# Bias of the up projection added to tile copies on ScalarE instead of by a matmul, with a new order of steps, in a fused adapter and attention kernel

## The chip, the cores and the metric

The kernel runs on one core of a Trainium2 chip. The metric is the device time of one execution in microseconds, lower is better; the figure compared is the median of several executions. A profile of one further execution goes with it.

## The reference, cut to what matters

Input x has 32 sequences of 32 tokens with 256 features. Each sequence has a role (1 or 2, clamped to 0 to 2), which picks the weights of three adapters. Four layers follow one another: an adapter (layer 0), attention and two MLPs (layer 1), an adapter (layer 2), an adapter (layer 3).

```python
def adapter(role, x, W_down, b_down, W_up, b_up, gamma, beta):
    h = gelu(einsum('bsh,bhk->bsk', x, W_down[role]) + b_down[role][:, None, :])
    u = einsum('bsk,bkh->bsh', h, W_up[role]) + b_up[role][:, None, :]
    y = x + u
    yn = (y - mean(y)) * rsqrt(var(y) + 1e-5)
    return yn * gamma[role][:, None, :] + beta[role][:, None, :]

def layer1(x, ...):
    attn = softmax((x @ Wq) @ (x @ Wk).T / 16)
    ao   = (attn @ (x @ Wv)) @ Wp + bp
    cms  = gelu(ao @ cW1 + cb1) @ cW2 + cb2 + one_hot(code)
    mod  = gelu(concat(ao, cms) @ mW1 + mb1) @ mW2 + mb2
    return clip(x + cms + mod, 0, 1)
```

## The kernel before, in words

The 1024 tokens are cut into 8 tiles of 128 tokens (4 sequences). The kernel sorts the sequences so that six tiles, the plain ones (0, 1, 2, 3, 6, 7), hold one role each; tiles 4 and 5, the mixed ones (MESSY), hold what is left and two roles, so they multiply with two sets of weights and mask the result. Layer 0 takes the tiles in the order 0, 1, 2, 3, 6, 7, 4, 5, layers 2 and 3 in the order of their numbers.

All engines walk through one list of steps, `plan()`. Each engine does its own part of a step and skips those in which it has none, so the list sets the order on every engine, and semaphores tie the engines together. The steps of an adapter tile are:

- load: gathered rows of x are transposed on TensorE into a bank and copied by ScalarE to xA (layer 0); in layer 2 VectorE clips x1T into xA. Layer 3 reads zB, which turn has written.
- down: TensorE puts x back into the bank in token order (two transposing matmuls, L741), adds b_up by a matmul with a one-hot matrix (L743), and computes the down product into the bank's other half (L748). ScalarE applies the Gelu with b_down (L940 for a plain tile, L945 for a mixed one), VectorE masks the mixed tiles (L1282).
- up: TensorE adds the up product to the bank (L764). VectorE takes statistics of a row (L1256, L1257), GpSimd raises the variance to the power -0.5 (L1514).
- center: VectorE subtracts the mean and scales, into yA (L1321).
- turn: TensorE transposes yA (L774), ScalarE applies gamma and beta into x1T or zB (L956, L968), for mixed tiles VectorE does it in two products (L1300, L1302).
- close and finish: in layer 3 VectorE writes the normed tile in two instructions (L1340, L1347), and GpSimd stores tiles 0 to 5 by an indirect DMA (L1529), SyncE and ScalarE store tiles 6 and 7.

The steps of layer 1 are split, project, scores, values, probs and mix (attention), hidden and outer (the MLPs, each matmul in three passes over high and low parts, L636 to L638), and weights (VectorE splits an MLP matrix into such parts, L1247, L1248). The hidden steps of the last phase, (3, 0) to (3, 7), and the outer steps (3, 0) to (3, 7) alternate with adapter tiles of layers 2 and 3. outer(3, 7) is the last matmul work of layer 1; VectorE then adds the result to x1T (L1432), from which tiles 6 and 7 of layer 2 start.

Adapter weights lie in two rings of four slots. SyncE fetches them in the order of its own program (L560, L563): for each slot it waits until the up step that last used it is done. For layers 2 and 3 it fetches in turn one pass of layer 2 and one of layer 3. The last two tiles have slots of their own (wd_last, wu_last).

For the bias matmul, VectorE builds the one-hot matrix `hot` for all eight tiles (first_hot and rest, L1137, L1189, L1191) and splits b_up of the three layers into high and low rows (first_bias for layer 0, L1216, L1218; late_biases for layers 2 and 3, L1230, L1232). SyncE loads those rows (bu_rows) ahead of everything but the first three loads, once GpSimd has cleared the tile (constants 3). chunk_vecs holds, per plain tile, the vectors of its role that ScalarE uses as bias and scale: b_down, gamma, beta; it comes from a matmul over vec_rows with 11 rows per role.

The program's names in the rows: bank is PSUM, stage the slots of MLP and attention matrices, x_tok gathered rows, g_h and g_l the high and low parts of the Gelu output, mvA and mvB the mean and variance of layers 0 and 2 and of layer 3.

Of the kernel before, what the change touches and what calls it, by code (L numbers as in the profile page):

```python
# [16 lines left out]
F32 = mybir.dt.float32  # L17
# [7 lines left out]
P = 128  # L25
# [25 lines left out]
PER_ROLE = 11  # L51
# [5 lines left out]
XSLOTS, YSLOTS, WSLOTS, TSLOTS = 3, 4, 4, 8  # L57

# [55 lines left out]
def plan():  # L114
# [7 lines left out]
        ("down", 0, 3), ("center", 0, 1), ("up", 0, 2), ("late_biases",), ("turn", 0, 0), ("center", 0, 2),
        ("up", 0, 3), ("load", 0, 7), ("seq_vecs",), ("turn", 0, 1), ("weights", 0, 0), ("center", 0, 3),
        ("load", 0, 4), ("down", 0, 6), ("down", 0, 7), ("turn", 0, 2), ("up", 0, 6), ("up", 0, 7), ("turn", 0, 3),
        ("center", 0, 6), ("split", 0, 0), ("load", 0, 5), ("down", 0, 4), ("center", 0, 7), ("token_tables",),
        ("turn", 0, 6), ("down", 0, 5), ("project", 0, 0), ("weights", 0, 1), ("turn", 0, 7), ("up", 0, 4),
        ("project", 0, 1), ("split", 1, 0), ("center", 0, 4), ("up", 0, 5), ("codes",), ("turn", 0, 4),
        ("center", 0, 5), ("scores", 0), ("values", 0, 0), ("probs", 0), ("values", 0, 1), ("turn", 0, 5),
        ("split", 1, 1), ("weights", 1), ("mix", 0), ("weights", 2), ("project", 1, 0), ("project", 1, 1),
        ("values", 1, 0), ("scores", 1), ("probs", 1), ("values", 1, 1), ("hidden", 0, 0), ("hidden", 0, 1),  # L130
        ("hidden", 0, 2), ("hidden", 0, 3), ("hidden", 0, 4), ("weights", 3), ("mix", 1), ("hidden", 0, 5),
# [5 lines left out]
        ("down", 2, 0), ("down", 2, 1), ("hidden", 3, 1), ("load", 2, 2), ("up", 2, 0), ("center", 2, 0),  # L137
# [1429 lines left out]
```

## Time and profile before

| | us |
|---|---|
| median of 3 runs | 202.34 |
| lowest, highest | 200.64, 202.97 |
| the profiled execution | 198.34 |
| its span, first to last instruction | 196.6 |

The profiled execution is one more run than the three. Its time holds 1.74 us ahead of and behind the span. The profile names for every instruction its start, its length and what ended the idle time before it. The recorded ends of matmuls are modelled: in the rows of time their lengths overlap, while the chain counts a step from start to start.

### The profile page before, as it was taken

What the parts mean: (1) busy time and instruction counts of PE and PEld (TensorE: products, weight loads), DVE (VectorE), ACT (ScalarE), POOL (GpSimd) and SP (SyncE); (2) the same over time, 40 slices, a digit from 0 to 9 for tenths busy, and PEclk for the clock granted to TensorE, in tenths of its full rate; (3) what the DMA queues carried; (4) which work ended last, traced back from release to release, by engine and by line L of the source; (5) the groups of instructions that cost most, each with busy time, mean ns of one, the idle gap of its engine ahead of it and who ended that gap; (6) DMA issues with size and microseconds to landing.
All of it is one profiled execution on the core that took longest, in us unless ns stands there. A gap on an engine that the chain in (4) does not pass through costs nothing.

```text
span 196.6 us, 3109 instructions
## 1 busy us (share of the span) xinstructions
PE 184.1 (94%) x1031; PEld 157.7 (80%) x1031; DVE 114.4 (58%) x283; ACT 80.7 (41%) x164; POOL 44.2 (22%) x74
## 2 busy tenths in 40 slices
PE   7877999989999999999999999999999999999960
PEld 7755878878988888778888888888888989999840
DVE  2994998989648807983193522041442146569972
ACT  0733656544698405672045543003546242222420
POOL 8472848200000006000140000000110012234552
PEclk9999999999999999999999999999999999999995
DMA  3687389996300230330000060000100005433002
GB/s 110 224 243 242 97 259 294 245 312 187 107 3 8 100 107 0 107 110 0 0 0 3 0 196 18 0 0 3 55 0 0 3 0 141 125 85 107 28 27 80
DMA packets 18585, 17.82 MB, mean 91 GB/s; under 512 B 2049, under 2 KB 16970, under 8 KB 18570
## 3 DMA queue, kind: packets, MB, share of 16 engines
q1 hardware_dynamic: 16720, 14.60, 24.3%
q0 software_dynamic: 1024, 2.37, 4.5%
q10 hardware_dynamic: 826, 0.67, 1.1%
q8 instruction: 8, 0.13, 0.3%
q14 instruction: 7, 0.06, 0.1%
HBM read 16.58 MB, written 1.05 MB: 90 GB/s over the span
## 4 chain that ended last, share of the span: by engine, by line
PE 79%; DVE 8%; DMA 5%; issue 3%; ACT 2%; POOL 1%; ACTq 0%; DVEq 0%; POOLq 0%
PE bank L636 20%; PE bank L638 19%; PE bank L637 19%; PE bank L748 5%; PE bank L764 5%; DMA stage<-in_L_cond_Wq 2%; PE bank L741 2%; PE bank L815 2%; PE bank L804 2%; DMA x_tok<-in_x,from_row_i 2%; PE bank L774 1%; DVE yA L1321 1%; PE bank L743 1%; DMA out<-yB,from_row_i 1%; DVE cms_l L1423 1%
## 5 line engine op out<-in xcount | busy, mean ns | idle before, releaser
L1402 DVE TENSOR_TENSOR g_l<-g_full,g_h 128x512 fp32r<-128x512 f32 x32 | 21.8, 690 | 36.1 <-ACT g_h L1028 36.0
L1025 ACT ACTIVATE g_full<-bank,vecs 128x512 f32<-128x512 f32 x32 | 22.1, 691 | 43.5 <-PE bank L638 39.9
L1514 POOL TENSOR_TENSOR mvA<-mvA,power 128x1 f32<-128x1 f32 x16 | 9.4, 589 | 72.0 <-DVE mvA L1257 72.0
L1028 ACT ACTIVATE g_h<-bank,vecs 128x512 fp32r<-128x512 f32 x32 | 22.0, 686 | 0.0
L1541 POOL TENSOR_TENSOR x1T<-x1T,cms_full 128x512 f32<-128x512 f32 x4 | 6.0, 1497 | 57.4 <-DVE cms_full L1417 57.3
L636 PE MATMUL bank<-g_h,mw_h 128*128 128x256 f32 (+1 forms) x48 | 16.0, 334 | 0.0
L638 PE MATMUL bank<-g_h,mw_l 128*128 128x256 f32 (+1 forms) x48 | 15.3, 318 | 0.0
L637 PE MATMUL bank<-g_l,mw_h 128*128 128x256 f32 (+1 forms) x48 | 15.3, 318 | 0.0
L636 PE MATMUL bank<-ao_h,mw_h 128*128 128x512 f32 x32 | 13.1, 411 | 0.0
L636 PE MATMUL bank<-ao_h,cw_h 128*128 128x512 f32 x32 | 12.8, 400 | 0.1
L638 PE MATMUL bank<-ao_h,mw_l 128*128 128x512 f32 x32 | 12.5, 391 | 0.0
L637 PE MATMUL bank<-ao_l,mw_h 128*128 128x512 f32 x32 | 12.5, 390 | 0.0
L638 PE MATMUL bank<-cms_h,mw_l 128*128 128x512 f32 x32 | 12.5, 390 | 0.0
L638 PE MATMUL bank<-ao_h,cw_l 128*128 128x512 f32 x32 | 12.5, 390 | 0.0
L636 PE MATMUL bank<-cms_h,mw_h 128*128 128x512 f32 x32 | 12.5, 390 | 0.0
L637 PE MATMUL bank<-ao_l,cw_h 128*128 128x512 f32 x32 | 12.5, 390 | 0.0
L636 PE MATMUL bank<-g_h,cw_h 128*128 128x512 f32 x32 | 12.5, 389 | 0.0
L638 PE MATMUL bank<-g_h,cw_l 128*128 128x512 f32 x32 | 12.5, 389 | 0.0
L637 PE MATMUL bank<-cms_l,mw_h 128*128 128x512 f32 x32 | 12.5, 389 | 0.0
L637 PE MATMUL bank<-g_l,cw_h 128*128 128x512 f32 x32 | 12.4, 389 | 0.0
L1321 DVE TENSOR_SCALAR yA<-bank,mvA 128x256 f32<-128x256 f32 x16 | 8.6, 540 | 3.1 <-POOL mvA L1514 2.8
L1417 DVE TENSOR_TENSOR cms_full<-bank,target 128x512 f32<-128x512 f32 x4 | 2.8, 692 | 12.9 <-PE bank L638 12.9
(265 smaller groups left out, 442.8 us busy)
## 6 DMA issues: line engine op xcount, KB each, us to landing
stage<-in_L_cond_mW SPq DMA_DIRECT2D x6, 512.0 KB
stage<-in_L_cond_cW SPq DMA_DIRECT2D x4, 512.0 KB
wdA<-in_L_cond_W_down SPq DMA_DIRECT2D x14, 128.0 KB
wuA<-in_L_cond_W_up SPq DMA_DIRECT2D x14, 128.0 KB
wdB<-in_L_cond_W_down SPq DMA_DIRECT2D x12, 128.0 KB, 2.5
wuB<-in_L_cond_W_up SPq DMA_DIRECT2D x12, 128.0 KB, 2.8
wd_last<-in_L_cond_W_down SPq DMA_DIRECT2D x4, 128.0 KB, 2.3
wu_last<-in_L_cond_W_up SPq DMA_DIRECT2D x4, 128.0 KB, 2.5
```

The costliest lines, as they stand in the source:

```text
L636: pe.matmul(dst, w[0], x[0], start=first, stop=False)
L637: pe.matmul(dst, w[0], x[1], start=False, stop=False)
L638: return pe.matmul(dst, w[1], x[0], start=False, stop=last)
L741: pe.matmul(bank[b][:, m * P:(m + 1) * P], x[:, m, :], ident[:, :], start=(m == 0), stop=False, is_transpose=True, skip_group_check=True)
L748: mm = pe.matmul(bank[b][:, D + part * P:D + (part + 1) * P], wd[:, k, :], x[:, k, :], start=False, stop=(k == KD - 1), skip_group_check=True)
L764: mm = pe.matmul(dst, h[:, part, :], wu[:, :], start=False, stop=(part == len(turns) - 1), skip_group_check=True)
L1025: act.activation(g_full[n % 2][:, 0:width], bank[b][:, 0:width], ACT.Gelu, bias=bias)
L1028: act.activation(g[0][:, j, 0:width], bank[b][:, 0:width], ACT.Gelu, bias=bias).then_inc(g_high, 1)
L1321: dve.tensor_scalar(yA[k][:, :], bank[chain_bank(layer, c)][:, 0:D], mvA[:, k, 0:1], mvA[:, k, 2:3], ALU.subtract, ALU.mult).then_inc(norm ...
L1402: dve.tensor_tensor(g[1][:, j, 0:width], g_full[n % 2][:, 0:width], g[0][:, j, 0:width].bitcast(F32), ALU.subtract).then_inc(g_ready, 1)
L1514: pool.tensor_tensor(mv[:, k, 2:3], mv[:, k, 1:2], power[:, :], ALU.pow).then_inc(done, 1)
L1541: pool.tensor_tensor(half, half, cms_full[:, m, :], ALU.add).then_inc(sum_ready, 1)
```

## The change

1. Plain tiles no longer get b_up by a matmul. ScalarE writes a copy of the tile with b_up added (`shift`: two activations of 128 x 128, bias from chunk_vecs) into new tiles rA (layers 0 and 2) and rB (layer 3), three slots each. In layer 0 it reads the transposed x in the bank, behind the copy to xA, in layer 2 xA, in layer 3 zB, behind its own writing of zB in turn. A slot waits for the TensorE step that last read it.
2. On TensorE, down of a plain tile is only the down product; the two transposing matmuls now read rA or rB and stand in up, ahead of the up product and behind the wait for the Gelu.
3. Mixed tiles keep the transposing matmuls and the bias matmul in down. `hot` is built for them alone; first_hot and first_bias are gone, and late_biases treats all three layers.
4. vec_rows has 17 rows per role instead of 11; the six new ones are b_up. chunk_vecs, seq_vecs and vecs grow with it, and both matmuls over vec_rows wait for six more small loads.
5. SyncE loads Wp first, then the small rows, then the weights of tiles 0, 1, 2, 3, 6, 7 of layer 0, then the first MLP matrix (piece 0) and bu_rows.
6. `plan()` has a new order.

```diff
+BU = {0: 11, 2: 13, 3: 15}
+PER_ROLE = 17
...
             def load(layer, c):
...
+                take(b, *((xA_ready, n + 1) if c in MESSY else (rA_ready, like_done(0, c))))
...
             def down(layer, c):
...
+                plain = c not in MESSY
+                if not plain:
+                    pe.wait_ge(bu_ready, 1)
+                    pe.wait_ge(hot_ready, 1)
+                    for m in range(KD):
+                        pe.matmul(bank[b][:, m * P:(m + 1) * P], x[:, m, :], ident[:, :], start=(m == 0), stop=False,
+                                  is_transpose=True, skip_group_check=True)
+                    pe.matmul(bank[b][:, 0:D], hot[:, c - MESSY[0], :], bu[:, (0, 2, 3).index(layer), :], start=False,
+                              stop=True, skip_group_check=True)
...
             def up(layer, c):
...
+                if c not in MESSY:
+                    r, ready, n, back = shifted(layer, c)
+                    pe.wait_ge(ready, n)
+                    for m in range(KD):
+                        tr = pe.matmul(bank[chain_bank(layer, c)][:, m * P:(m + 1) * P], r[:, m, :], ident[:, :],
+                                       start=False, stop=False, is_transpose=True, skip_group_check=True)
+                    tr.then_inc(back, 1)
...
+            def shift(layer, c, x):
+
+                r, ready, n, back = shifted(layer, c)
+                if n > RSLOTS:
+                    act.wait_ge(back, n - RSLOTS)
+                for m in range(KD):
+                    ins = act.activation(r[:, m, :], x[m], ACT.Identity,
+                                         bias=chunk_vecs[:, BU[layer] + m, full_column(c):full_column(c) + 1])
+                ins.then_inc(ready, 1)
...
-            def first_bias():
-
-                dve.wait_ge(bu_in, 16)
-                dve.tensor_copy(bu_high[:, 0, :], bu_rows[:, 0, :]).then_inc(bu_high_ready, 1)
...
+                dve.wait_ge(bu_in, 3 * 16)
+                dve.tensor_copy(bu_high[:, :, :], bu_rows[:, :, :]).then_inc(bu_high_ready, 1)
...
     return [
...
-        ("close", 3, 1), ("finish", 3, 0), ("load", 2, 5), ("down", 2, 4), ("up", 3, 2), ("outer", 3, 5),
...
+        ("up", 3, 1), ("load", 2, 5), ("turn", 2, 3), ("close", 3, 1), ("finish", 3, 1), ("outer", 3, 5),
```

TensorE, right behind the last matmul of outer(3, 7), before. xA_150 and xA_148 are tiles 6 and 7 of layer 2, zB_158 and wdB_135 tile 3 of layer 3, wuA_128 and wuA_129 the up weights of tile 5 of layer 2.

```order
L741 MATMUL bank<-ident,zB_158 128x128 x2
L743 MATMUL bank<-bu,hot 128x256
L748 MATMUL bank<-zB_158,wdB_135 128x128 x2
L774 MATMUL bank<-ident,yA_154 128x128 x2
L764 MATMUL bank<-wuA_128,hA_152 128x256
L764 MATMUL bank<-wuA_129,hA_152 128x256
L764 MATMUL bank<-wuB_139,hB_161 128x256
L741 MATMUL bank<-ident,xA_150 128x128 x2
L743 MATMUL bank<-bu,hot 128x256
L748 MATMUL bank<-xA_150,wd_last_8_140 128x128 x2
```

The same place now.

```order
L786 MATMUL bank<-wuA_130,hA_151 128x256
L786 MATMUL bank<-wuA_131,hA_151 128x256
L786 MATMUL bank<-wuA_128,hA_152 128x256
L786 MATMUL bank<-wuA_129,hA_152 128x256
L763 MATMUL bank<-zB_158,wdB_135 128x128 x2
L763 MATMUL bank<-xA_150,wd_last_8_140 128x128 x2
L763 MATMUL bank<-xA_148,wd_last_9_141 128x128 x2
L796 MATMUL bank<-ident,yA_154 128x128 x2
L780 MATMUL bank<-ident,rB_240 128x128 x2
L786 MATMUL bank<-wuB_139,hB_161 128x256
```

The up products of tile 4 (wuA_130, wuA_131) have come behind the last outer step. The three down steps have neither transposing nor bias matmuls, and up of tile 3 of layer 3 has the transposing ones, from rB_240.

VectorE from the clipping of tile 7 of layer 2 (xA_148) on, before. zB_159 is tile 4 of layer 3, yA_155 and yB_167 are tile 5 of layer 2 and tile 3 of layer 3.

```order
L1268 TENSOR_SCALAR xA_148<-x1T 128x256
L1300 TENSOR_TENSOR zB_159<-bank,seq_vecs 128x256
L1302 TENSOR_TENSOR zB_159<-zB_159,seq_vecs 128x256
L1256 BN_STATS statsA<-bank 128x6
L1257 BN_AGGR mvA<-statsA 128x2
L1256 BN_STATS statsB<-bank 128x6
L1257 BN_AGGR mvB<-statsB 128x2
L1321 TENSOR_SCALAR yA_155<-bank,mvA 128x256
L1340 ISA
L1340 SCALAR_TENSOR_TENSOR yB_167<-bank,mvB,table_gamma_172 128x256
```

The same place now. yA_154 is tile 4 of layer 2, yB_166 tile 2 of layer 3.

```order
L1298 TENSOR_SCALAR xA_148<-x1T 128x256
L1284 BN_STATS statsA<-bank 128x6
L1285 BN_AGGR mvA<-statsA 128x2
L1352 TENSOR_SCALAR yA_154<-bank,mvA 128x256
L1371 ISA
L1371 SCALAR_TENSOR_TENSOR yB_166<-bank,mvB,table_gamma_172 128x256
L1352 TENSOR_SCALAR yA_155<-bank,mvA 128x256
L1331 TENSOR_TENSOR zB_159<-bank,seq_vecs 128x256
L1333 TENSOR_TENSOR zB_159<-zB_159,seq_vecs 128x256
L1284 BN_STATS statsB<-bank 128x6
```

The centring of tile 4 and the first product of tile 2 now stand between xA_148 and zB_159; before, both stood ahead of the last outer step's result. In the whole stretch from the clipping of tile 6 to the statistics of tile 4 of layer 3 there are now one statistics pair, one centring, one first and one last product more than before.

SyncE from its third load to the first adapter weights, before.

```order
L536 DMA role_col_i<-in_itok_B_1546 32x1
L581 DMA bu_rows<-in_L_cond_b_up 6x1x256 x3
L583 DMA stage_122<-in_L_cond_Wp 128x2x256
L548 DMA stage_123<-in_L_cond_cW 128x1024
L587 DMA vec_rows<-in_L_cond_gamma 3x128 x2
L587 DMA vec_rows<-in_L_cond_beta 3x128 x2
L554 TENSOR_LOAD chunk_role_i
```

The same place now.

```order
L548 DMA role_col_i<-in_itok_B_1546 32x1
L591 DMA stage_122<-in_L_cond_Wp 128x2x256
L595 DMA vec_rows<-in_L_cond_b_up 3x128 x2
L595 DMA vec_rows<-in_L_cond_gamma 3x128 x2
L595 DMA vec_rows<-in_L_cond_beta 3x128 x2
L595 DMA vec_rows<-in_L_cond_b_up 3x128 x4
L566 TENSOR_LOAD chunk_role_i
```

bu_rows and the 512 KB matrix (cW) have gone behind the weights of six tiles.

## Rows read from the trace of the kernel before

**Rows 1.** The page, part 1: busy us, share of the span, instructions.
```profile
PE 184.1 (94%) x1031; PEld 157.7 (80%) x1031; DVE 114.4 (58%) x283; ACT 80.7 (41%) x164; POOL 44.2 (22%) x74
```

**Rows 2.** Busy time by stage: stretch, its length, busy of each engine.
```profile
12.00:51.85 39.85, 36.40 (x248) 31.58 (x249) 33.11 (x99) 19.46 (x49) 14.80 (x19) 1.00 0.79 232
51.85:130.60 78.75, 78.60 (x354) 64.71 (x353) 40.09 (x56) 35.61 (x57) 5.99 (x4) 1.00 0.13 42
130.60:176.90 46.30, 46.30 (x291) 41.53 (x290) 19.31 (x47) 16.63 (x35) 6.58 (x10) 1.00 0.15 44
176.90:196.60 19.70, 12.94 (x88) 11.04 (x86) 14.10 (x39) 4.59 (x13) 8.91 (x13) 0.89 0.19 60
```

**Rows 3.** The chain that ended last: start, us, what (x2: pieces of one step).
```profile
133.50 0.22 PE bank L741 x2
133.72 0.12 PE bank L743
133.84 0.44 PE bank L748 x4
...
157.48 0.86 PE bank L764 x4
...
187.50 0.74 issue
188.23 1.04 POOL out L1529
189.30 0.59 POOL mvB L1514
```

**Rows 4.** TensorE in order of time: start, length, line, operands.
```profile
14.01 0.41 PE L719 MATMUL bank<-ident,x_tok 128*128 128x128 f32 x2 [0.47 <-issue]
...
176.80 0.38 PE L741 MATMUL bank<-ident,zB 128*128 128x128 f32 x2
```

**Rows 5.** SyncE's fetches for a released slot, and the landing of wd_last.
```profile
170.37 0.37 SPq L560 DMA_DIRECT2D wdB<-in_L_cond_W_down  x1
171.37 0.38 SPq L560 DMA_DIRECT2D wdA<-in_L_cond_W_down  x1
...
DMA to landing us min/median/max: 2.1/2.3/2.6
```

**Rows 6.** VectorE behind the last outer step, in order of time.
```profile
177.52 0.49 DVE L1268 TENSOR_SCALAR xA<-x1T 128x256 f32<-128x256 f32 x2
178.00 0.42 DVE L1300 TENSOR_TENSOR zB<-bank,seq_vecs 128x256 f32<-128x256 f32 x1
...
178.87 0.43 DVE L1256 BATCH_NORM_STATS2 statsA<-bank 128x6 f32<-128x256 f32 x1
179.45 0.39 DVE L1256 BATCH_NORM_STATS2 statsB<-bank 128x6 f32<-128x256 f32 x1
...
180.22 0.54 DVE L1321 TENSOR_SCALAR yA<-bank,mvA 128x256 f32<-128x256 f32 x1 [0.15 <-POOL mvA L1514]
180.68 0.48 DVE L1340 SCALAR_TENSOR_TENSOR yB<-bank,mvB,table_gamma 128x256 f32<-128x256 f32 x1
...
185.56 0.43 DVE L1256 BATCH_NORM_STATS2 statsB<-bank 128x6 f32<-128x256 f32 x1
```

**Rows 7.** GpSimd's second of two stores in a row.
```profile
177.23 0.98 POOL L1529 DMA_INDIRECT out<-yB,from_row_i  x1 [0.30 <-issue]
```

**Rows 8.** ScalarE and VectorE: activations, and VectorE's one-hot and bias passes.
```profile
15.75 0.37 ACT L923 COPY xA<-bank 128x256 f32<-128x256 f32 x1 [1.59 <-PE bank L719]
17.31 0.62 ACT L940 ACTIVATE hA<-bank,chunk_vecs 128x128 f32<-128x128 f32 x2 [1.19 <-PE bank L748]
...
185.78 1.50 ACT L968 ACTIVATE zB<-bank,chunk_vecs 128x128 f32<-128x128 f32 x4 [0.67 <-PE bank L774]
...
22.00 0.28 DVE L1191 CAST hot<-hot_col 128x256 fp32r<-128x256 f32 x1
23.22 0.72 DVE L1230 CAST bu_high<-bu_rows 128x512 fp32r<-128x512 f32 x1
23.97 0.75 DVE L1232 SCALAR_TENSOR_TENSOR bu<-bu_high,low_row,bu_rows 128x512 fp32r<-128x512 f32 x1
```

More of the change, by code:

```diff
@@ L122, in plan @@
[L122 to L126, printed above, removed]
@@ new lines, in plan @@
+        ("turn", 0, 0), ("up", 0, 2), ("weights", 0, 0), ("load", 0, 6), ("up", 0, 3), ("center", 0, 2),
+        ("down", 0, 6), ("load", 0, 7), ("seq_vecs",), ("late_biases",), ("turn", 0, 1), ("center", 0, 3),
+        ("up", 0, 6), ("down", 0, 7), ("load", 0, 4), ("turn", 0, 2), ("up", 0, 7), ("token_tables",),
+        ("turn", 0, 3), ("center", 0, 6), ("split", 0, 0), ("load", 0, 5), ("center", 0, 7), ("down", 0, 4),
+        ("down", 0, 5), ("turn", 0, 6), ("project", 0, 0), ("weights", 0, 1), ("up", 0, 4), ("turn", 0, 7),
@@ L150, in plan @@
-        ("finish", 3, 5), ("close", 3, 6), ("down", 3, 7), ("finish", 3, 6), ("up", 3, 7), ("close", 3, 7),
-        ("finish", 3, 7),
+        ("down", 2, 2), ("turn", 2, 1), ("hidden", 3, 5), ("down", 3, 0), ("hidden", 3, 6), ("load", 2, 3),
+        ("outer", 3, 0), ("up", 2, 2), ("up", 3, 0), ("hidden", 3, 7), ("outer", 3, 1), ("down", 2, 3),
+        ("close", 3, 0), ("center", 2, 2), ("outer", 3, 2), ("up", 2, 3), ("down", 3, 1), ("turn", 2, 2),
+        ("outer", 3, 3), ("center", 2, 3), ("finish", 3, 0), ("outer", 3, 4), ("load", 2, 4), ("down", 3, 2),
@@ L284, in build @@
         role_row_of = place("role_row_of", [P, 1], F32)
-        hot_col = place("hot_col", [P, FULL], F32)
         hot_rest = place("hot_rest", [P, 2 * WB], F32)
-        hot = place("hot", [P, WIN, P], F32R)
+        hot = place("hot", [P, len(MESSY), P], F32R)
+        rA = [place(f"rA{i}", [P, KD, P], F32) for i in range(RSLOTS)]
         x1T = place("x1T", [P, KD, N], F32)
@@ L327, in build @@
         cms_full = place("cms_full", [P, KD, HALF], F32, scratch)
+        rB = [place(f"rB{i}", [P, KD, P], F32, scratch + 4 * KD * P * i) for i in range(RSLOTS)]
         at[0] = max(at[0], early_end)
@@ L748, in down @@
                         mm = pe.matmul(bank[b][:, D + part * P:D + (part + 1) * P], wd[:, k, :], x[:, k, :],
-                                       start=False, stop=(k == KD - 1), skip_group_check=True)
+                                       start=(plain and k == 0), stop=(k == KD - 1), skip_group_check=True)
                 mm.then_inc(done, 1)
@@ L972, in turn2 @@
                 ins.then_inc(zB_ready, 1)
+                if c == 0:
+                    act.wait_ge(cms_ready, 2 * KD)
+                    act.wait_ge(sum_ready, 2 * KD)
+                act.wait_ge(zB_ready, like_done(2, c))
+                shift(3, c, [zB[c % XSLOTS][:, m, :] for m in range(KD)])
             def values(h, q):
@@ L1267, in load @@
                 dve.wait_ge(downA_ps, i - XSLOTS + 1)
+                if c >= XSLOTS and c - XSLOTS not in MESSY:
+                    dve.wait_ge(rA_ready, like_a(2, c - XSLOTS))
                 dve.tensor_scalar(xA[i % XSLOTS][:, :, :], x1T[:, :, c * P:(c + 1) * P], 0.0, 1.0,
```

123 lines of the change are left out of this document (59 added, 64 removed).

## The prediction, made before the changed kernel ran

> **What bounds the kernel now.** I read the busy shares first, then busy time by stage, then the chain that ended last, then the rows in time around the two places where TensorE waits. TensorE is busy 94% of the span, VectorE 58%, ScalarE 41% [rows 1]. By stage it falls apart [rows 2]. From 12 to 51.85 us (adapters of layer 0, attention) TensorE is busy 36.40 of 39.85 us, VectorE 33.11: 3.45 us idle. From 51.85 to 130.60 it is full (78.60 of 78.75), from 130.60 to 176.90 as well (46.30 of 46.30). After that, where only adapter tiles are left, it is busy 12.94 of 19.70 us, and VectorE 14.10. So a matmul taken out before 176.9 pays in full, one taken out behind it only if the chain there runs over TensorE. That chain, over the last 10 us, alternates VectorE, GpSimd's store of one tile and GpSimd's power for the next: 0.74 us from a finished tile to the store, the store, and only then the power at 189.30 [rows 3]. The granted clock is 1.00 in the three long stages.
>
> **The profiled run and the median.** The profiled execution took 198.34 us, 1.74 more than its span of 196.6; the median of the runs is 202.34. I sum differences against the span and add them to the median.
>
> **TensorE's part.** A plain tile loses its bias matmul: 0.12 us in the chain, 18 of them (6 plain tiles, 3 layers), 2.16 us. The two transposing matmuls (0.22 a pair) stay, but stand in up instead of down, and there behind the wait for the Gelu, so they hide under nothing: 0.34 less ahead of each Gelu, 0.22 more behind it [rows 3].
>
> From the first matmul of hidden(3,0) to the end of outer(3,7) at 176.80 [rows 4] TensorE is full, so the sum counts: 7 plain down steps there without bias, 7 x 0.12 = 0.84, and the two up matmuls of tile 4 of layer 2 now stand behind outer(3,7), 0.86 [rows 3]. The last outer ends 0.84 + 0.86 = 1.70 us earlier, of which only 0.84 is work gone.
>
> Could weights be late there? SyncE asks for a slot's weights only once the slot's last up is done, in a fixed order, and layer 3's first fetch for tile 5 (behind up(3,2)) stands ahead of layer 2's second for tile 5: 1.00 us between the two [rows 5]. Now only down(2,4) (0.22 + 0.12 + two weight pairs of 0.44 = 1.22) and outer(3,6) (12 matmuls as wide as the bias one, 1.44) stand between up(3,2) and down(2,5), whose second half is needed 0.65 + 1.22 + 1.44 + 0.22 + 0.12 + 0.44 = 4.09 us after up(3,2) began [rows 3]. The fetch is issued 0.65 + 0.16 (end of the step to the result, 0.38 less 0.22 [rows 3, 4]) + 1.00 = 1.81 after that and lands 2.3 later (2.1 to 2.6) [rows 5]: 4.11. Just in time; I take 0, and up to 0.3 for the upper end.
>
> **VectorE behind the last outer.** Steps between starts [rows 6]: statistics 0.58 (178.87 to 179.45), centring 0.46, two products for a mixed tile 0.87 (178.00 to 178.87), xA 0.25, first product of a finished tile 0.48, last the same form, mask 0.40 (it is of the form of those products, 0.42 long). From the end of outer(3,7) to the statistics of tile 4 of layer 3 it is 185.56 - 176.80 = 8.76 now. In the new order VectorE starts with x1T and xA, waits for up(2,4) until 1.07 (0.86, the same 0.16, and the hand-over), and then has in a row: 5 statistics (2.90), xA (0.25), 4 centrings (1.84), 2 first products (0.96), 2 mixed tiles (1.74), 2 last products (0.96), 2 masks (0.80): 9.45. Each of TensorE's and ScalarE's results for it comes earlier than its turn by my count (for example the Gelu of tile 4 at about 7.6, its mask's turn at 8.8). So the statistics start at 10.52, 1.76 later against the end of the outer. VectorE was waiting before where it now works: statistics and centring of tile 4 of layer 2, a first and a last product were done before the outer ended.
>
> GpSimd then has two stores (tiles 2 and 3) right ahead of the power of tile 4. A store takes 1.04 [rows 3], the next starts 0.30 behind it and takes 0.98 [rows 7]. Tile 2 is finished at 8.32, its store starts 0.8 later (0.74 and the hand-over, [rows 3]), at 9.12, the second at 10.46 and is over at 11.44; the power could have started about 0.7 behind the statistics (0.58 and the hand-over), at 11.24: 0.20 late. From there on the order is the one of before to the end. Tail: -1.70 + 1.76 + 0.20 = +0.26.
>
> **The start.** ScalarE gets 18 pairs of 128-wide activations. It has not run this form; the nearest is the Gelu with a bias, a pair 0.62 [rows 8], which I take; the dearer bound is the scaled pair, 1.50 for four, 0.75 [rows 8]. 18 x 0.62 = 11.2 us on an engine busy 80.7: no bound in itself. In layer 0 they stand between the copy of x and the Gelu. Down is 0.34 shorter and up 0.22 longer, -0.12 once. Then VectorE leads: it is busy 33.11 of the stage's 39.85 us [rows 2], and its pass over the late biases ends just where the next centring starts [rows 8]. The early hot and bias work (four instructions) went from a stretch where it ran ahead; what counts is the copy of hot_col, 0.28 gone, and the late bias pass, now 768 wide instead of 512: 0.72 + 0.75 become half as much again, +0.73 [rows 8]. Start: -0.12 - 0.28 + 0.73 = +0.33, and since TensorE is full from project on, it stays. Bounds: nothing below -3.45 (all the idle time of the stage, [rows 2]) and nothing above 6 x 0.62 = 3.7, if every pair stood in the chain. SyncE: the first matrix (512 KB) goes behind the weights of six tiles, b_up gets six small row copies ahead of the two vector transposes; the queue starts Wp at once instead of behind the wait for bu_rows, so these are issued before it waits for the roles, and cost nothing. Weights(3) ahead of hidden(0,0) puts two VectorE instructions before the first g_l, which outer(0,0) needs only eight hidden steps later: 0.
>
> Sum: +0.26 + 0.33 = +0.6: 202.34 + 0.6 = 202.9 us (a profiled span of about 197.2).
>
> **Rivals.**
> B, TensorE's sum. If VectorE's queue behind the last outer packs tighter than rows 6 say, or the end hangs on TensorE after all, the 18 matmuls pay in full: 202.34 - 2.16 = 200.2. For it: the tail's chain does touch TensorE at several tiles. Against: 5 us and more of TensorE idle in the tail [rows 2].
> C, queued transfers. At the start ScalarE stands idle 1.59 us before xA of the second tile and 1.19 before the first Gelu, though the matmuls it names had long been issued [rows 8]. If that is the 512 KB matrix in front of x and the weights, it goes with the new order: up to 2.78 less the new pair, 2.16. Then 202.9 - 2.16 = 200.7. Against: the transpose of that tile starts at 14.01 [rows 4], so its data was there. The Trainium skill, DMA: Bandwidth & Descriptors, section Queues, rings and completion order, says that a transfer's semaphore lands only after every earlier write of that DMA engine, across its queues: by that rule the new order would free the gathers' semaphores, and the time is this rival's. No row here shows it directly.
> D, ScalarE's queue, slower. It is in order, and each new pair stands ahead of the next copy, Gelu or x1T. If in layer 0 five of six pairs hold up the chain, 5 x 0.62 = 3.1 on top of mine less the 0.33 that VectorE would then hide: 202.9 + 3.1 - 0.3 = 205.7. It decides from the point where ScalarE's idle time ahead of a Gelu is under 0.62; now it is 1.19 and 1.59 at the first tiles [rows 8], and ScalarE is busy 19.46 of 39.85 us [rows 2]. The Trainium skill, TensorE: Matmul & The Clock Gate, section on the array's architecture, calls ScalarE's queue strictly first in, first out; by it nothing overtakes such a pair, and this rival stands.
>
> **How the numbers follow.** Mine 0.46, B 0.17, C 0.15, D 0.17, 0.05 for something else. About 1% (2 us) is what a measurement of this kernel tells from no change, its runs lying 2.3 us apart. Faster by over 1% (under 200.3): most of B, a third of C, 0.23. Slower (over 204.4): D and the upper end of mine, 0.21. Within: 0.56. The range 199.5 to 206.0 takes in B, C and D; mine alone is 201.6 to 204.2.
>
> **What would show it.** Right: outer(3,7) ends 1.4 us earlier in the span (1.70 less 0.33); VectorE without a gap over 0.3 us from 1.1 us after it until the statistics of tile 4; project(0,0) 0.3 us later in the span; the new pair takes 0.62 to 0.75 us. Wrong: ScalarE named ahead of TensorE's gaps before 30 us (D), those two gaps gone (C), a tail shorter than 20 us behind the last outer (B), a stall at down(2,5).

## The result, and the profile after

| | before | after |
|---|---|---|
| median of 20 runs each, taken on one chip | 200.36 us | 203.61 us |
| lowest, highest | 198.38, 203.10 | 201.57, 208.63 |
| ratio after to before, 95% interval | | 1.0171 (1.0137 to 1.0205) |
| the profiled execution, its span | 198.34, 196.6 | 202.39, 200.4 |

The changed kernel is slower by 1.7%, 3.25 us between the medians, where the forecast said +0.6. The 202.34 on which the forecast stood was the median of three runs only; twenty runs of the same kernel give 200.36. Ratios, here and below, compare only the executions in the faster of the two states that an execution can be in, while medians and extremes are of all of them, so the two need not agree to the last digit.

Part 1 of the page of the changed kernel answers to [rows 1].

```profile
PE 184.3 (92%) x1013; PEld 156.9 (78%) x1013; DVE 112.9 (56%) x278; ACT 91.6 (46%) x200; POOL 44.9 (22%) x74
```

ScalarE is 10.9 us busier and TensorE has 18 matmuls fewer, as planned. Yet TensorE is busy 0.2 us longer, not 2.2 us shorter: some of its steps took more time each. The busy time by stage shows where (the stretches are cut at the same steps as in [rows 2]; columns: stretch, its length, busy of each engine, granted clock, DMA share, GB/s).

```profile
12.00:54.96 42.96, 38.09 (x246) 32.24 (x246) 34.22 (x101) 23.02 (x63) 15.56 (x19) 0.96 0.81 232
54.96:133.70 78.74, 78.58 (x354) 64.74 (x353) 40.17 (x56) 35.56 (x57) 6.00 (x4) 1.00 0.13 41
133.70:178.66 44.96, 44.74 (x280) 39.97 (x279) 17.36 (x42) 21.74 (x51) 6.20 (x9) 1.00 0.16 48
178.66:200.40 21.74, 13.27 (x88) 11.21 (x86) 15.50 (x44) 7.18 (x21) 9.90 (x13) 0.91 0.16 49
```

Against [rows 2] the first stretch is 3.11 us longer, the second equal, the third (46.18 us from hidden(3,0) to the end of outer(3,7) before, cut at 130.62 and 176.80) 1.22 shorter, the last (19.8 before) 1.94 longer: +3.8 together. The granted clock of the first is 0.96, where it was 1.00. That of the last (0.91, before 0.89) falls only behind TensorE's last step and costs nothing: it is 1.00 until 192 us before and until 196 after, and that step starts at 190.06 and 192.13.

**The start.** TensorE in order of time, before, then after.

```profile
6.03 1.07 PE L692 MATMUL bank<-ident,stage 128*128 128x128 f32 x8 [0.77 <-DMA stage<-in_L_cond_Wq]
...
17.73 1.13 PE L764 MATMUL bank<-wuA,hA 128*128 128x256 f32 x4 [0.32 <-ACT hA L940]
...
30.97 0.47 PE L636 MATMUL bank<-x_h,wqk_h 128*128 128x512 f32 x1 [0.17 <-issue]
```

```profile
6.88 1.06 PE L706 MATMUL bank<-ident,stage 128*128 128x128 f32 x8 [1.34 <-DMA stage<-in_L_cond_Wq]
...
14.96 1.35 PE L763 MATMUL bank<-xA,wdA 128*128 128x128 f32 x8
16.15 0.38 PE L733 MATMUL bank<-ident,x_tok 128*128 128x128 f32 x2
18.61 0.46 PE L780 MATMUL bank<-ident,rA 128*128 128x128 f32 x2 [2.08 <-ACT hA L980]
18.89 1.04 PE L786 MATMUL bank<-wuA,hA 128*128 128x256 f32 x2
...
33.55 0.47 PE L650 MATMUL bank<-x_h,wqk_h 128*128 128x512 f32 x1 [0.18 <-issue]
```

Three things are to be seen. Wq lands later: the first transposes start at 6.88, 0.85 later than before. Then TensorE stands idle for 2.08 us until the first Gelu. And behind that wait an up step takes 1.04 us instead of the 0.60 of an undisturbed one: the clock has fallen from 2.4 to 1.2 GHz. The same view as above for two short stretches, behind the wait and in it, has the granted clock at 0.50 and 1.00:

```profile
18.90:22.30 3.40, 3.40 (x14) 2.50 (x12) 1.65 (x5) 1.33 (x6) 0.88 (x2) 0.50 0.65 202
16.00:18.60 2.60, 0.53 (x5) 0.29 (x4) 0.61 (x2) 0.47 (x3) 0.86 (x1) 1.00 0.95 287
```

project(0,0) starts at 33.55 us instead of 30.97, 2.58 later. ScalarE at the same place, after:

```profile
15.43 0.63 ACT L944 ACTIVATE rA<-bank,chunk_vecs 128x128 f32<-128x128 f32 x2
18.19 0.62 ACT L980 ACTIVATE hA<-bank,chunk_vecs 128x128 f32<-128x128 f32 x2 [2.13 <-remote]
```

The down product for the first Gelu was issued at 14.96 and the second one ended by 16.3. ScalarE, free since 16.06, started the Gelu at 18.19, and the profile names no engine ("remote") as the releaser. [Rows 8] held the same gap in two pieces, 1.59 and 1.19.

Another 0.5 us is lost between project(0,0) and the first mix. ScalarE and VectorE each copy half of the scores; VectorE, after:

```profile
40.78 0.43 DVE L1333 TENSOR_TENSOR x1T<-x1T,seq_vecs 128x256 f32<-128x256 f32 x1
41.13 0.54 DVE L1352 TENSOR_SCALAR yA<-bank,mvA 128x256 f32<-128x256 f32 x1
41.58 0.56 DVE L1401 COPY dots<-bank 32x128 f32<-32x128 f32 x2
```

ScalarE's copy starts at 41.09, VectorE's 0.49 later, behind the products of a mixed tile and a centring; before, both started at 38.46.

**Around the last outer steps.** TensorE and SyncE, after.

```profile
172.18 0.38 PE L780 MATMUL bank<-ident,rB 128*128 128x128 f32 x2
...
176.67 0.71 PE L763 MATMUL bank<-xA,wdA 128*128 128x128 f32 x4 [0.22 <-DMA wdA<-in_L_cond_W_down]
...
178.66 1.89 PE L786 MATMUL bank<-wuA,hA 128*128 128x256 f32 x8
```

```profile
174.00 0.56 SPq L572 DMA_DIRECT2D wdA<-in_L_cond_W_down  x1
```

up(3,2) starts at 172.18; the weights for the second half of down(2,5) are asked for 1.82 us later and arrive 2.67 us after that, 0.39 us too late (176.67 against 176.28, when the first half is done).

**The tail.** VectorE and GpSimd, after; [rows 3, 6, 7] are the same places before.

```profile
179.72 0.43 DVE L1284 BATCH_NORM_STATS2 statsA<-bank 128x6 f32<-128x256 f32 x1
...
186.15 0.48 DVE L1378 SCALAR_TENSOR_TENSOR yB<-yB,mvB,table_beta 128x256 f32<-128x256 f32 x1
...
188.64 0.43 DVE L1284 BATCH_NORM_STATS2 statsB<-bank 128x6 f32<-128x256 f32 x1
```

```profile
187.44 1.63 POOL L1560 DMA_INDIRECT out<-yB,from_row_i  x1 [0.40 <-issue]
189.37 0.98 POOL L1560 DMA_INDIRECT out<-yB,from_row_i  x1 [0.31 <-issue]
190.35 0.59 POOL L1545 TENSOR_TENSOR mvB<-mvB,power 128x1 f32<-128x1 f32 x1
```

The statistics of tile 4 of layer 3 start 9.98 us behind the last outer (8.76 before) and the power 11.69 behind it (9.51 before, 186.31 less 176.80), held by the second store. From there to the end the tail gives 0.24 us back.

### The profile page after: what moved, and what is told of

Its sections match the earlier page's. It is cut to its first block, busy times and chain, and to the rows that moved or that the text cites. A ratio compares the mean times of both kernels' runs of the same rounds, so it can differ in the third digit from the quotient of the medians.

```text
span 200.4 us, 3123 instructions
## 1 busy us (share of the span) xinstructions
PE 184.3 (92%) x1013; PEld 156.9 (78%) x1013; DVE 112.9 (56%) x278; ACT 91.6 (46%) x200; POOL 44.9 (22%) x74
## 4 chain that ended last, share of the span: by engine, by line
PE 72%; DVE 10%; DMA 5%; issue 4%; ACT 3%; POOL 2%; another core or an unknown queue 1%; SPq 0%; ACTq 0%; DVEq 0%; POOLq 0%
PE bank L650 19%; PE bank L652 18%; PE bank L651 18%; PE bank L786 4%; PE bank L763 3%; DMA stage<-in_L_cond_Wq 3%; PE bank L837 2%; PE bank L826 2%; DMA wdA<-in_L_cond_W_down 1%; PE bank L720 1%; POOL out L1560 1%; DVE mw_l L1276 1%; PE bank L780 1%; PE bank L796 1%
## 5 line engine op out<-in xcount | busy, mean ns | idle before, releaser
L650 PE MATMUL bank<-g_h,mw_h 128*128 128x256 f32 (+1 forms) x48 | 15.7, 326 | 0.0
L650 PE MATMUL bank<-ao_h,cw_h 128*128 128x512 f32 x32 | 12.8, 399 | 0.2
L944 ACT ACTIVATE rA<-xA,chunk_vecs 128x128 f32<-128x128 f32 x12 | 4.1, 393 | 16.0 <-DVE xA L1298 16.0
L1082 ACT CAST cms_h<-cms_full 128x512 fp32r<-128x512 f32 x4 | 2.5, 622 | 17.9 <-DVE cms_full L1448 9.7
```

The source lines that it names most:

```text
L650: pe.matmul(dst, w[0], x[0], start=first, stop=False)
L944: ins = act.activation(r[:, m, :], x[m], ACT.Identity, bias=chunk_vecs[:, BU[layer] + m, full_column(c):full_column(c) + 1])
```

## The experiments

My theory for the start at this point: the new order of loads makes Wq late, and the long wait for the first Gelu lets the clock fall. Rivals: the added pairs in ScalarE's queue, or the new order of steps. L numbers in rows are those of each run's own kernel.

**1. The moved work alone.** The changed kernel with both old orders: the steps of before without first_hot, of which two places stand here, and the loads of run 2.

```diff
-        ("chunk_vecs",), ("vectors",), ("load", 0, 0), ("fold", 1, 1), ("load", 0, 1), ("down", 0, 0),
+        ("chunk_vecs",), ("vectors",), ("sort_rest",), ("load", 0, 0), ("fold", 1, 1), ("load", 0, 1),
...
-        ("up", 3, 2), ("down", 2, 4), ("outer", 3, 6), ("down", 2, 5), ("outer", 3, 7), ("load", 2, 6), ("up", 2, 4),
+        ("close", 3, 2), ("finish", 3, 2), ("outer", 3, 6), ("down", 2, 5), ("outer", 3, 7), ("down", 3, 3),
```

> The changed kernel with the old order of steps and the old order of loads: only the work moved from TensorE to ScalarE is left of the change. Theory 1 (the start is lost to the new load order: Wq lands at 6.75 instead of 5.90 us, and then to a TensorE clock that falls because the first Gelu comes late): project(0,0) starts at 31.0 to 31.5 us, as before, the outer stretch is 0.84 us shorter, ratio to before 0.990 to 1.000. Theory 2 (ScalarE's queue: the added pairs hold up the Gelus of layer 0): project(0,0) still 2 us or more later, ratio 1.008 or more. Theory 3 (the order of steps makes the loss at the start): reads as theory 1 here, and differs in the next run.

Measured: median 199.56 against 199.81, ratio 1.005 (0.9995 to 1.0104).

```profile
6.28 1.07 PE L705 MATMUL bank<-ident,stage 128*128 128x128 f32 x8 [0.59 <-DMA stage<-in_L_cond_Wq]
...
31.63 0.47 PE L649 MATMUL bank<-x_h,wqk_h 128*128 128x512 f32 x1 [0.16 <-issue]
...
151.79 0.71 PE L762 MATMUL bank<-xA,wdA 128*128 128x128 f32 x4 [0.36 <-ACT zB L1007]
```

Wq is 0.25 late, though it is loaded as before: with the loads of before the wait for it ended anywhere from 6.00 to 6.46 in the seven traces of this case (runs 1, 2, 7 and 10 to 12 and the kernel before). project(0,0) is 0.66 late, so 0.41 us at the start belong to the moved work; the rest of the 2.58 does not. VectorE shows where they arise: the two passes over the late biases and then the next centring, in this run, and that centring in the kernel before, where the passes start at 23.22 [rows 8].

```profile
23.37 0.96 DVE L1258 CAST bu_high<-bu_rows 128x768 fp32r<-128x768 f32 x1
...
25.30 0.54 DVE L1351 TENSOR_SCALAR yA<-bank,mvA 128x256 f32<-128x256 f32 x1
```

```profile
24.64 0.54 DVE L1321 TENSOR_SCALAR yA<-bank,mvA 128x256 f32<-128x256 f32 x1
```

The wider passes take 1.93 us instead of 1.42, 0.51 more; ahead of them this run is 0.15 late, and behind them 0.66 until project(0,0).

From project to mix it takes 11.31 us, as before; every run with the new order there took 11.6 to 11.8. So that half microsecond is the order's. The moved work gains nothing either: the stretch of hidden(3,0) to outer(3,7) is only 0.23 us shorter. Taken step by step, TensorE saves 1.42 us of bias matmuls (seven), pays 0.56 more for the transposing ones (0.22 a pair where 0.14 was paid in down), and loses 0.64 around the wait for zB shown above, which ScalarE writes later with its longer queue. Its end is 0.4 longer (20.0 us against 19.6; here and in runs 3, 8 and 11 the stretches that begin or end with outer(3,7) are measured to the modelled end of its last matmul, 0.15 behind the start of the next step, which the table above takes: 21.6 for the changed kernel, and 45.1 for the stretch ahead). Between the two nothing is left.

**2. The old order of loads.**

```diff
+            sp.wait_ge(constants, 3)
+            for m, w in enumerate(("L0_cond_b_up", "L2_cond_b_up", "L3_cond_b_up")):
+                sp.dma_start(bu_rows[0:2 * R, m, :],
...
             sp.dma_start(square("p"), a["L1_cond_Wp"].rearrange("(k p) n -> p k n", p=P)).then_inc(square_in["p"], 16)
+            piece(0)
...
-                if n == 5:
-                    piece(0)
```

> The changed kernel with SyncE's old order of loads (bu_rows, Wp and piece 0 ahead of the small rows), new order of steps. Theory 1: the wait for Wq is over at about 5.9 instead of 6.75, project(0,0) starts 0.85 us earlier than in the changed kernel at least (32.7), and if the late Gelu goes too, at 31 to 31.5; ratio to before 1.003 to 1.013. Theories 2 and 3: no change against the changed kernel, ratio 1.017.

Measured: ratio 1.0157 (1.0049 to 1.0266).

```profile
6.12 1.06 PE L705 MATMUL bank<-ident,stage 128*128 128x128 f32 x8 [1.17 <-DMA stage<-in_L_cond_Wq]
...
32.66 0.47 PE L649 MATMUL bank<-x_h,wqk_h 128*128 128x512 f32 x1 [0.18 <-issue]
```

Wq is on time and project(0,0) 0.89 us earlier than in the changed kernel. That is the part of the loads, and all of it, for in this execution too the clock fell, at two waits of TensorE of 1.39 and 1.07 us. As the size of that part 0.85 is at the upper end: the six traces with the new loads and no wait added have 6.73 to 6.88, on average 0.6 behind the seven of run 1.

**3. The old order of steps from load(2,0) on.**

```diff
-        ("down", 2, 0), ("hidden", 3, 1), ("up", 2, 0), ("center", 2, 0), ("down", 2, 1), ("load", 2, 2),
+        ("load", 2, 0), ("load", 2, 1), ("hidden", 3, 0), ("down", 2, 0), ("down", 2, 1), ("hidden", 3, 1),
...
-        ("up", 3, 2), ("down", 2, 4), ("outer", 3, 6), ("down", 2, 5), ("outer", 3, 7), ("load", 2, 6), ("up", 2, 4),
+        ("turn", 2, 3), ("close", 3, 2), ("finish", 3, 2), ("outer", 3, 6), ("down", 2, 5), ("outer", 3, 7),
```

> The changed kernel with the old order of steps from load(2,0) on, new order ahead of it. Theory: the start stays as in the changed kernel (project(0,0) at 33.5); the 0.4 us stall at down(2,5) goes, the stretch from the end of outer(3,7) to the end of the span is 19.8 to 20.2 us instead of 21.7, while outer(3,7) ends 0.84 us earlier than before against hidden(3,0) instead of 1.22: together 1.1 to 1.5 us less than the changed kernel, ratio to before 1.010 to 1.012. Rival (the tail's order gives and takes the same): ratio 1.017 as the changed kernel.

Measured: median 202.05 of four runs, lowest 200.46 (the changed kernel's lowest: 201.57); too few runs for a ratio with an interval. TensorE in the profile:

```profile
18.50 0.44 PE L780 MATMUL bank<-ident,rA 128*128 128x128 f32 x2 [1.66 <-ACT hA L980]
...
32.22 0.47 PE L650 MATMUL bank<-x_h,wqk_h 128*128 128x512 f32 x1 [0.18 <-issue]
```

In that profile, 198.5 us of span, TensorE waited 1.66 us for the first Gelu instead of 2.08 and the clock did not fall, and project(0,0) stands at 32.22 with the new order ahead of it. Of the 1.33 us between that and 33.55, 0.11 are there already at the first up step (18.50 against 18.61). The fall is worth the other 1.22: from that step to project(0,0) it takes 13.72 here, 13.72 in run 4 and 13.71 in run 1, all without a fall, and 14.94 in the changed kernel and 14.86 in run 2, both with one of 3.4 us. It is not in every execution. The stall at down(2,5) is gone, and the rest behind the last outer takes 20.0 us instead of 21.6 (19.6 before). What is left of the tail's loss shows here; ScalarE, then TensorE:

```profile
187.94 0.69 ACT L944 ACTIVATE rB<-zB,chunk_vecs 128x128 f32<-128x128 f32 x2
188.54 0.79 ACT L1008 ACTIVATE zB<-bank,chunk_vecs 128x128 f32<-128x128 f32 x2
189.36 0.69 ACT L944 ACTIVATE rB<-zB,chunk_vecs 128x128 f32<-128x128 f32 x2
189.96 0.35 ACT L980 ACTIVATE hB<-bank,chunk_vecs 128x128 f32<-128x128 f32 x1
```

```profile
190.35 0.44 PE L780 MATMUL bank<-ident,rB 128*128 128x128 f32 x2 [1.67 <-ACT hB L980]
```

Two new pairs stand ahead of the Gelu of tile 6, and TensorE waits 1.67 us for it, where it waited 0.46 before.

**4. Filler matmuls in the wait for the first Gelu.**

```diff
-        ("sort_rest",), ("down", 0, 1), ("load", 0, 2), ("sort_codes",), ("fold_low", 1), ("up", 0, 0), ("up", 0, 1),
+        ("down", 0, 1), ("load", 0, 2), ("sort_codes",), ("fold_low", 1), ("warm", 4), ("up", 0, 0), ("up", 0, 1),
```

> The changed kernel with eight 128x128 filler matmuls on TensorE ahead of up(0,0), where it waits 2.1 us for the first Gelu. They compute nothing of the result. Theory 1: the granted clock stays at 1.00 between 18 and 24 us, the steps there take what they take at 2.4 GHz (0.60 for an up pair instead of 1.04), and project(0,0) starts 1.0 to 1.7 us earlier, ratio to before 1.008 to 1.012. Rival (the fallen clock is covered by VectorE and ScalarE, which set the pace there): same as the changed kernel, 1.017.

Measured: ratio 1.0114 (1.0006 to 1.0221), lowest 201.50.

```profile
16.70 1.06 PE L658 MATMUL bank<-warm 128*128 128x128 f32 x8
18.49 0.44 PE L780 MATMUL bank<-ident,rA 128*128 128x128 f32 x2 [0.74 <-ACT hA L980]
18.76 0.60 PE L786 MATMUL bank<-wuA,hA 128*128 128x256 f32 x2
...
32.21 0.47 PE L650 MATMUL bank<-x_h,wqk_h 128*128 128x512 f32 x1 [0.18 <-issue]
```

With a shorter gap the up step takes 0.60 again, and project(0,0) stands where it stood in run 3 without a fall: 1.34 us earlier than in the changed kernel. Alone the filler proves little, since run 3 has no fall without it; the two together give the price of a fall. The fillers do not bring the Gelu nearer, and the lowest time is no better than the changed kernel's 201.57, which had no fall either by its mean clock (0.989).

**5. Wp no earlier than before.**

```diff
+            sp.wait_ge(constants, 3)
             sp.dma_start(square("p"), a["L1_cond_Wp"].rearrange("(k p) n -> p k n", p=P)).then_inc(square_in["p"], 16)
```

> The changed kernel with one wait added in SyncE: Wp is issued only when GpSimd has cleared bu_rows (constants 3, about 3.2 us), as before. Theory 1a (what delays Wq is Wp, issued 3.2 us earlier than before and moved at the same time as Wq, Wk): the wait for Wq ends at 5.9 to 6.3 us. Rival 1b (the six small loads of b_up rows, or the place of piece 0, delay it): 6.8 us as in the changed kernel.

Measured: one run, 203.28.

```profile
6.13 1.06 PE L707 MATMUL bank<-ident,stage 128*128 128x128 f32 x8 [0.44 <-DMA stage<-in_L_cond_Wq]
```

The early issue is what makes Wq late: with Wp issued at 3.23 instead of 2.19 us, beside the 512 KB of Wq and Wk, the wait ends 0.75 earlier, and the new place of the first MLP matrix, kept here, has no part in it. The wait held back the small loads behind Wp too (from 2.66 to 3.65), so the run does not part the two; the sizes, 256 KB against 1.5 KB for each of the six new ones, speak for Wp. The run as a whole was no faster, because the clock fell for 6.8 us at a wait of 2.93 us.

**6 and 7. Weights held back,** in the changed kernel and in the kernel before.

```diff
+                if n == 3:
+                    sp.wait_ge(hA_ready, 1)
                 adapter_weights(0, n)
```

> The changed kernel with one wait added in SyncE: the weights of the fourth tile and all after them are asked for only once the first Gelu is done. Theory Q (the first Gelu comes 2.1 us late because the results it waits for are reported late while loads queue up): the Gelu starts before 17.3 us instead of 18.2, TensorE's wait there is under 1.2 us, the clock does not fall; project(0,0) at 31 to 31.8 instead of 33.5, ratio to before 1.003 to 1.010. Rival (the late Gelu has nothing to do with the loads behind it): the Gelu at 18.1 to 18.2, and the weights held back may cost something more, ratio 1.017 or above.

> The kernel before with the same wait added. Theory Q: ScalarE's two idle stretches of 1.59 and 1.19 us ahead of the second xA and of the first Gelu shrink to under 1 us together, project(0,0) 1 to 2 us earlier than 31.0, ratio 0.990 to 0.997. Rival: same as before, or slower by up to 1 us where the held weights come late.

Measured: ratio 1.0247 (1.019 to 1.0303) and 0.9963 (0.9932 to 0.9994). The Gelu starts at 17.82 and at 17.66 (Wq was 0.4 later in the latter than in [rows 8]'s run), so with no weights asked for between 12.8 and 18.3 us it is still 1.97 us late in run 6, and in run 7 ScalarE's two idle pieces are 1.54 and 1.13 where they were 1.59 and 1.19: the theory that queued weights delay it falls. Run 6 lost more: VectorE, which had waited 3.18 us for the MLP matrix that is asked for behind the held weights, came late with a centring, TensorE waited 3.41 us until 29.16, and the clock fell at 30 us. In run 7 something else is better: its ten runs lie between 198.15 and 198.78, those of before beside them between 198.36 and 202.83. Part of it is the clock: all ten have a mean granted clock of 0.989 or above, while three of those thirteen have 0.981 or below (200.14, 202.81 and 202.83). Yet three more of the thirteen took 199.32 to 200.80 at 0.988 or above, so that is not all, and why the held weights steady it stays open.

**8. Another order of the last fetches.**

```diff
-            for n in range(WSLOTS, SLOTTED):
-                adapter_weights(2, n)
-                adapter_weights(3, n)
+            for layer, n in ((2, 4), (3, 4), (2, 5), (2, 6), (2, 7), (3, 5), (3, 6), (3, 7)):
+                adapter_weights(layer, n)
```

> The changed kernel with SyncE's order of the last eight fetches changed: both fetches for tile 5 of layer 2 stand ahead of the three of layer 3 that wait for layer 3's up steps. Theory (the stall at down(2,5), 0.4 to 0.9 us, comes from its second fetch queued behind layer 3's): the stall goes, hidden(3,0) to the end of outer(3,7) takes 44.6 to 44.8 us instead of 45.1, the rest behind it stays 21.6 us. Rival: the transfer itself is slow, the stall stays.

Measured: one run, 202.70; in this execution the clock was at half for 6.8 us at the start. TensorE and SyncE:

```profile
176.62 1.05 PE L762 MATMUL bank<-xA,wdA 128*128 128x128 f32 x8
```

```profile
166.87 0.37 SPq L572 DMA_DIRECT2D wdA<-in_L_cond_W_down  x1
171.50 0.37 SPq L572 DMA_DIRECT2D wdB<-in_L_cond_W_down  x1
```

The last fetch for layer 2 (wdA) now stands 4.6 us ahead of the next one of layer 3, all eight matmuls of down(2,5) run in one piece, the stretch is 44.6 us instead of 45.1, and behind it nothing changes (21.6). The stall came from the place in SyncE's queue.

**9 and 10. Gathers held back,** in the changed kernel (the fourth to sixth, as shown) and in the kernel before (the fifth and sixth, i == 4). In every trace so far ScalarE's long wait ahead of the first Gelu (in run 5 ahead of the copy of x before it) ended 1.1 to 1.3 us behind the end of GpSimd's sixth gather, wherever that stood.

```diff
-                for c in EARLY:
+                for i, c in enumerate(EARLY):
+                    if i == 3:
+                        pool.wait_ge(hA_ready, 1)
                     gather(c)
```

> The changed kernel with GpSimd's gathers of x for the fourth, fifth and sixth tile held back until the first Gelu is done. Theory G (TensorE's results are reported late as long as gathers run: in all traces so far updates come one at a time, some 0.7 us apart, until 1.1 to 1.3 us behind the last gather): the third gather ends at about 13.1 us, so the first Gelu starts at 16.0 to 16.6 instead of 18.2, right behind the pair for the second tile. Rival (something else at a fixed time, a code load or the profiler): Gelu still at 17.8 to 18.2. The time itself may get no better, since the held gathers come later and disturb another stretch.

> The kernel before with the fifth and sixth gather held back until the first Gelu is done. Theory G: the first Gelu starts 1 to 2 us earlier than 17.3; what the start keeps of it until project(0,0) is at most 1 us, because the held gathers then run beside the next tiles: ratio to before 0.993 to 1.002. Rival: Gelu at 17.3 as before, ratio 1.000.

Measured: one run of 203.48, and ratio 0.9908 (0.9859 to 0.9957). ScalarE in run 9, TensorE in run 9, ScalarE in run 10:

```profile
15.62 0.63 ACT L944 ACTIVATE rA<-bank,chunk_vecs 128x128 f32<-128x128 f32 x2
16.14 0.78 ACT L980 ACTIVATE hA<-bank,chunk_vecs 128x128 f32<-128x128 f32 x2
```

```profile
21.73 0.41 PE L733 MATMUL bank<-ident,x_tok 128*128 128x128 f32 x2 [3.63 <-DMA x_tok<-in_x,from_row_i]
```

```profile
14.85 0.38 ACT L923 COPY xA<-bank 128x256 f32<-128x256 f32 x1
15.41 0.37 ACT L940 ACTIVATE hA<-bank,chunk_vecs 128x128 f32<-128x128 f32 x1 [0.18 <-PE bank L748]
```

This is the cause of the late Gelu. With three gathers fewer in flight the Gelu starts the moment ScalarE is free, 2.05 us earlier than in the changed kernel; with two fewer, in the kernel before, it starts 1.9 us earlier, and project(0,0) stands at 30.05 instead of 30.97. In run 9 the fourth tile's rows then came too late (3.63 us of waiting and a fallen clock), so nothing was gained; in run 10 that wait was 0.46. Run 10's ratio is better than expected (0.993 to 1.002). Its lowest time is 1.00 us under that of before, about the 0.92 of project(0,0); the rest goes with the clock, for all its ten runs have a mean of 0.986 or above, of the 23 of before beside them 11 have 0.985 or above.

**11 and 12. The moved work only where TensorE is full,** alone and together with run 10's edit: b_up on ScalarE for tiles 0 to 3 of layers 2 and 3, all else as before.

```diff
+MOVED = (0, 1, 2, 3)
...
+                moved = layer and c in MOVED
```

> The kernel before, its order of steps and loads kept, with b_up added by ScalarE only for tiles 0 to 3 of layers 2 and 3, where TensorE is full; layer 0 and tiles 6 and 7 keep the bias matmul. Theory (a bias matmul taken out of the full stretch is worth 0.12 us, and the losses of the change lie at the start and in the tail): the outer stretch is up to 0.84 us shorter, less a wait of 0.4 us for zB seen in the run with the work moved alone, start and tail as before; ratio 0.995 to 0.999. Rival (the pairs cost elsewhere what they save): 1.000 or above.

> The kernel before with both edits that helped: the fifth and sixth gather held back until the first Gelu, and b_up added by ScalarE for tiles 0 to 3 of layers 2 and 3 only. If the two are independent (one acts ahead of project(0,0), the other between hidden(3,0) and outer(3,7)), the lowest times are 0.2 us below the 197.34 to 197.50 of the first alone: 197.1 to 197.3, ratio to before 0.985 to 0.992. If the longer table of vectors (15 rows per role instead of 11) delays the start, nothing is added: 197.4 or above.

Measured: 0.9947 (0.9903 to 0.9991) and 0.9899 (0.9854 to 0.9944), lowest 198.16 and 196.44. Run 11's tail is 19.5 us (19.6 before), so the 0.4 us of runs 1 and 3 were the pairs of tiles 6 and 7. Its stretch from hidden(3,0) to outer(3,7) is 0.15 us shorter than before, since TensorE waits for zB again:

```profile
153.55 0.71 PE L767 MATMUL bank<-xA,wdA 128*128 128x128 f32 x4 [0.33 <-ACT zB L1008]
```

A ratio of 0.9947 is more than that explains. Its own lowest time is 0.18 under the lowest of before, which fits; but how often the clock fell does not account for the rest. With a mean clock of 0.989 or above, five of its twelve runs took 198.16 to 198.66 and eight of the 23 of before 198.34 to 199.46, so it is ahead at like clock too, and why stays open (its own profile has TensorE idle for 3.31 us at the start, and a fall). Runs 10 and 12 beat both kernels. Their intervals overlap, so they can't be told apart, though run 12's lowest, 196.44, is below the 197.1 to 197.3 expected.

## Why the prediction was right or wrong

The forecast of the difference was wrong: +0.6 expected, +3.25 measured. That the stated range held 203.6 is luck. Around the better base of 200.36 it would be 197.5 to 204.0 and hold it just, by the upper end that rival D's price had set, and D is not what happened; the narrower range of the forecast's own sum, 201.6 to 204.2, would be 199.6 to 202.2 and miss it. Point by point:

- **The tail: near in sum.** Forecast -1.70 + 1.76 + 0.20 = +0.26; measured -1.22 + 1.94 = +0.72, of which 0.39 is the stall of the next point. The row of VectorE instructions from 179.72 to 188.64 is the forecast's, without a gap over 0.3 us, 8.92 us for a forecast 9.45, so the statistics came 1.22 later and not 1.76. The two stores in front of the power cost more: the statistics would have allowed it at 189.39, it ran at 190.35, 0.96 late instead of 0.20, 0.25 of it because the two stores were over later than counted (the first took 1.63), 0.5 because the statistics were earlier than the count. With the 0.24 that the end gives back the errors nearly cancel (1.96 forecast, 1.94 measured), which is luck too.
- **Weights just in time: the right place, the wrong side.** Issue 1.81 forecast, 1.82 measured; need 4.09 and 4.10; the landing was 2.67 instead of 2.3. The term was taken as 0 with 0.3 as the upper end and measured 0.39, in runs 2 and 4 about 0.9, where the landing took 3.1 and 3.2. Run 8 shows the queue to be its cause.
- **TensorE's part: right per matmul.** 0.12 us a tile net (0.34 less, 0.22 more), seven tiles. What was not seen is that ScalarE's longer queue makes zB late: in the old order 0.64 of the 0.86 goes there (run 1).
- **The start: wrong.** The step that failed is "Start: -0.12 - 0.28 + 0.73 = +0.33". Measured +3.11: 0.85 for Wq (runs 2 and 5), 1.22 for the fallen clock (runs 1, 3 and 4 against the changed kernel and run 2), 0.53 of the new order between project and mix, and 0.51 that remain until project. Those are near the 0.41 of the moved work in run 1, and so near the forecast's size and its mechanism: VectorE's wider passes over the late biases, forecast at 0.73, cost 0.51 there. The failed sentences are "the queue starts Wp at once instead of behind the wait for bu_rows, so these are issued before it waits for the roles, and cost nothing", which looked at SyncE's own queue and not at what moves beside Wp, and the assumption that the granted clock of 1.00 in [rows 2] would stay. The fallen clock varies between executions, of before too. Of the changed kernel's 20 runs five have a mean granted clock of 0.985 or above and took 201.57 to 201.94, the other fifteen 0.981 or below and 202.39 or more; of the 66 runs of the kernel before that were taken beside the experiments 35 have 0.985 or above. So it lifts both medians. Without it, by the lowest times, the difference is 201.57 - 198.38 = 3.2 us; the profile of run 4, which has no fall, puts 1.73 of it at the start and 1.27 behind hidden(3,0), with a stall of 0.94.
- **Rival C, queued transfers: wrong in its price, near in its place.** The gaps of 1.59 and 1.19 us did have a cause among the transfers, but not the 512 KB matrix, which was out of the way in the new order, nor the weights (runs 6 and 7): it was the gathers. The Trainium skill, DMA: Bandwidth & Descriptors, section Queues, rings and completion order, tells of the semaphores of transfers, which land behind earlier writes. Here a result of TensorE came late, not only those of transfers, and of that the section says nothing; the measurement decides.
- **Rival D, ScalarE's queue: wrong at the start, right at the end.** Its condition (less than 0.62 us of idle time ahead of a Gelu) was met in the tail, at the Gelu of tile 6 with 0.41 of waiting, and at zB. At the start the pairs were covered by the wait that the gathers made. The sign given for it, ScalarE named ahead of a gap of TensorE before 30 us, did come (2.08 us), but the Gelu named there stood behind the gathers and not behind a pair: the sign did not tell the two apart. The pair took 0.63 us from a bank and 0.69 from SBUF, inside the bounds of 0.62 to 0.75.
- **Rival B, TensorE's sum: wrong.** No execution came near 200.2.

## What to carry to other kernels

A load issued earlier can delay whatever moves beside it (here Wq by 0.6 to 0.85 us): look at what lands first on the path, not only at the queue into which the load is put. A wait at which the matmul engine stands for 2 us can cost twice, once for the wait and once for the steps behind it at half the clock (here 1.22 us); so look at what covers such a wait before it is taken out (here the bias matmuls and transposes of down; that taking them out made the wait so long is argued, no run shows it alone). And before work is moved to an idle engine, find the two or three results of that engine for which others wait: it was idle 59% of the time, and late for zB and for the Gelu of tile 6.

## What the runs showed that I had not expected

- While GpSimd's gathers run, TensorE's results reach ScalarE up to 2 us late. The trace's own record of updates has them arrive one or two at a time, 0.6 to 0.7 us apart (at 15.1, 15.7, 16.4 and 17.1 in the kernel before), then in a burst 1.1 to 1.3 us behind the end of the last gather. That the gathers cause it is shown by runs 9 and 10; by what path is open.
- The clock fell to half for 3.4 or 6.8 us in seven of the fourteen profiles within the first 34 us. In six of them TensorE had the longest idle pieces of all (1.95 in run 8, 2.08 in the changed kernel, 2.93 to 3.63 in runs 5, 6, 9 and 11); the seventh, run 2, had 1.39 and 1.07 close together. Without a fall went 1.34 and 0.98 in run 1, 1.66 in run 3 and 1.82 (the wait for Wq) in run 4. One fall of 3.4 us ahead of project(0,0) costs 1.22 us.
- Two transposing matmuls cost 0.14 us in a row of other matmuls of the same tile and 0.22 on their own in up.
